# A transformer layer and a Mamba layer on one core: a new order inside the Mamba pair step, and the weighting of x on GpSimd

## What is computed

```python
gate, hbc, dt = split(hidden @ in_proj_w)
hbc = silu(causal_conv4(hbc) + conv_b)          # x (4096 channels), B, C (128 each)
dt  = softplus(dt + dt_bias);  dA = dt * -exp(A_log);  cum = cumsum(dA)   # inside a block
scores = (C_i . B_j) * exp(cum_i - cum_j) * dt_j          # i >= j
Y_diag = scores @ x
states = sum_l exp(cum_last - cum_l) * dt_l * B_l x_l     # of each block
state  = exp(cum_last) * state + states                   # carried from block to block
Y_off  = exp(cum_l) * C_l @ state_before
hidden = (Y_diag + Y_off + D * x) * silu(gate)
out    = rmsnorm(hidden) * norm_w @ out_proj_w
```

## Time and profile before

| | |
|---|---|
| median of 3 runs | 1969.08 us (1966.39 to 1969.34) |
| the profiled execution's own time | 1966.99 us |
| its span, first to last instruction | 1965.2 us |
| mean granted TensorE clock | 0.994 |
| busy: TensorE, VectorE, ScalarE, GpSimd | 1911.9, 1532.6, 1310.2, 830.7 us |
| DMA, mean over the span | 122 GB/s |

### The profile page before, as it was taken

How to read it: one execution, slowest core, us unless ns; L and a number is a source line. 1 busy time by engine, 2 the same in 40 slices (tenths; PEclk the granted TensorE clock), 3 DMA queues, 4 the chain that set the end, 5 groups by cost and what they waited for, 6 DMA issues and landing times.

```text
span 1965.2 us, 43300 instructions
## 1 busy us (share of the span) xinstructions
PE 1911.9 (97%) x12642; PEld 1607.5 (82%) x12642; DVE 1532.6 (78%) x2860; ACT 1310.2 (67%) x2983; POOL 830.7 (42%) x997
## 2 busy tenths in 40 slices
PE   7999999999999999999999999999999999999998
PEld 7888778888888968888878886888888888788886
DVE  6886678888788468888878836888888883688886
ACT  4663389999555148888845514888875551588885
POOL 2210268888200016777710001777770000177776
PEclk9999999999999999999999999999999999999999
DMA  6330356656422114444422211544442221244442
GB/s 231 120 120 1 124 162 207 203 193 208 134 75 85 52 46 156 146 155 148 164 77 84 75 62 35 168 146 157 146 153 86 91 62 49 83 146 156 146 153 78
DMA packets 122051, 239.86 MB, mean 122 GB/s; under 512 B 10832, under 2 KB 48912, under 8 KB 121872
## 3 DMA queue, kind: packets, MB, share of 16 engines
q1 hardware_dynamic: 122000, 239.18, 37.2%
HBM read 198.37 MB, written 37.62 MB: 120 GB/s over the span
## 4 chain that ended last, share of the span: by engine, by line
PE 71%; issue 20%; DVE 5%; ACT 2%; POOL 1%; DMA 0%; POOLq 0%; DVEq 0%; ACTq 0%
PE bank L695 31%; PE bank L965 12%; PE bank L952 6%; PE bank L941 5%; PE bank L932 4%; PE bank L924 3%; PE both L695 2%; PE bank L845 2%; PE bank L802 2%; DVE conv_acc L1428 1%; PE both L802 1%; PE bank L772 1%; PE bank L777 1%; PE bank L854 0%; ACT bank L1166 0%
## 5 line engine op out<-in xcount | busy, mean ns | idle before, releaser
L695 PE MATMUL bank<-xn_r,w_r 128*128 128x512 f32 x2268 | 610.6, 409 | 4.2 <-issue 3.2
L695 PEld LDWEIGHTS bank<-xn_r,w_r 128*128 128x128 f32 x2268 | 413.1, 189 | 104.9 <-issue 27.2
L1428 DVE SCALAR_TENSOR_TENSOR conv_acc<-bank,conv_sb,conv_acc 128x511 f32<-128x511 f32 (+2 forms) x408 | 304.3, 746 | 39.0 <-ACT conv_acc L1161 5.3
L570 POOL TENSOR_TENSOR rstd<-var_eps,minus_half 128x4 f32<-128x4 f32 (+2 forms) x12 | 9.7, 808 | 627.9 <-DVE var_eps L1357 627.9
L965 PE MATMUL bank<-wo_n,place 128*128 128x256 f32 x1024 | 255.1, 392 | 1.6 <-DVE place L1606 1.6
L1344 DVE TENSOR_TENSOR place_r<-bank,place_r 128x512 fp32r<-128x512 f32 (+1 forms) x320 | 186.7, 632 | 76.2 <-ACT place_r L1084 76.2
L1084 ACT ACTIVATE place_r<-bank 128x512 fp32r<-128x512 f32 (+1 forms) x320 | 159.2, 556 | 126.0 <-PE bank L695 98.7
L591 POOL TENSOR_TENSOR shared<-shared,c_t 128x768 f32<-128x768 f32 x128 | 234.4, 1831 | 6.6 <-ACT shared L1262 6.6
L965 PEld LDWEIGHTS bank<-wo_n,place 128*128 128x128 f32 x1024 | 184.0, 189 | 43.2 <-issue 21.2
L613 POOL TENSOR_TENSOR sumsq<-sumsq,place 128x512 f32<-128x512 f32 x127 | 161.9, 1275 | 114.8 <-ACT place L1150 114.8
L695 PE MATMUL bank<-place_r 128*128 128x512 f32 (+3 forms) x960 | 188.9, 337 | 8.4 <-DVE place_r L1344 6.0
(11 more groups left out here) (163 smaller groups left out, 3597.0 us busy)
## 6 DMA issues: line engine op xcount, KB each, us to landing
place_r<-cum_rows SPq DMA_DIRECT2D x128, 512.0 KB, 3.9
w_r<-pair_split SPq DMA_DIRECT2D x96, 512.0 KB, 3.7
w_r<-qkv_split SPq DMA_DIRECT2D x48, 512.0 KB, 4.0
pair_split<-w_r SPq DMA_DIRECT2D x32, 512.0 KB, 4.0
qkv_split<-w_r SPq DMA_DIRECT2D x16, 768.0 KB, 3.9
w_r<-qkv_split SPq DMA_DIRECT2D x48, 256.0 KB, 3.2
wo_n<-out_split SPq DMA_DIRECT2D x96, 128.0 KB, 3.6
raw<-in_w_pair SPq DMA_DIRECT2D x32, 256.0 KB, 3.9
```

What stands on the lines that cost most here:

```text
L695: ins = mm(out, lhsT=w(a), rhs=m(b), start=(start and i == 0), stop=(stop and i == 2), **kw)
L1428: stt(out=conv_acc[:, back:W], in0=src[:, 0:W - back], scalar=conv_sb[:, ch, TAPS - 1 - back:TAPS - back], in1=conv_acc[:, back:W], op0=AL ...
```

## The change

TensorE's order in a pair becomes project_gate(n+1), project_x(n+2), turn_x(n+1), project_out(n-1), in_block(n), off_block(n), make_states(n+1). The transposed x goes to one bank, ScalarE copies it to `x_raw` in SBUF, and GpSimd forms from it both x_w (`weigh_x`, now with the decays times dt) and x_dt (the new `weigh_dt`); VectorE's `weighted` is gone. The growth factors are made once per sequence by one exponential, saved to memory, and loaded spread over the partitions for each pair (`grow_save`, `grow_load`); ScalarE's `growth` is gone. The orders on ScalarE, VectorE, GpSimd and SyncE are rewritten to go with it; the raw weights of the first sequence are now split three pairs ahead of pair n in place of two. `c_grow` gets memory of its own. The diff, cut; lines with @@ name the engine:

```diff
-        c_grow = shared[:, n_mix + n_xw:n_mix + n_xw + 4 * (W - P)].rearrange("p (a h w) -> p a h w", a=2, h=2)
+        x_raw = shared[:, f_at + 4 * W:f_at + 5 * W].rearrange("p (t q) -> p t q", t=NT)
+        c_grow = sb("c_grow", [P, 2, 2, W - P])
...
@@ SyncE @@
+            def grow_save(b):
+                sp.wait_ge(s_grow_ev, b + 1)
+                sp.dma_start(grow_rows[bass.ds(b, 1), :, :].rearrange("b h w -> h (b w)"), square[0:MH, :]).then_inc(s_grow_saved, 16)
+                sp.wait_ge(s_grow_saved, b * 16 + 16)
+            def grow_load(b, n, par):
+                if not first(b) or not isinstance(n, int) or n > 0:
+                    sp.wait_ge(s_off_done, b * NPAIR + n)
+                sp.dma_start(c_grow[:, par, :, :], grow_rows[bass.ds(b, 1), bass.ds(n * 2, 2), P:W]
+                             .to_broadcast([P, 2, W - P])).then_inc(grow_in[par], 16)
...
-                    sp.wait_ge(s_grow_ev, b * NPAIR + n - 1)
+                    sp.wait_ge(s_span, b * NPAIR + n - 1)
...
-                with sp.Fori(1, NPAIR // 2 - 1) as i:
+                with sp.Fori(1, NPAIR // 2 - 2) as i:
                     for par in range(2):
-                        pair_save(i * 2 + par, par)
-                        pair_load(i * 2 + par + 2, par)
+                        grow_load(0, i * 2 + par + 1, 1 - par)
+                        pair_save(i * 2 + par + 1, 1 - par)
+                        pair_load(i * 2 + par + 3, 1 - par)
                         spread_load(0, i * 2 + par + 2, par)
                         out_save(i * 2 + par - 2, par)
                         out_load(i * 2 + par, par)
...
                         pair_fetch(i * 2 + par + 2, par)
                         spread_load(b, i * 2 + par + 2, par)
                         out_fetch(b, i * 2 + par, par)
+                        grow_load(b, i * 2 + par + 1, 1 - par)
...
@@ GpSimd @@
             def weigh_x(b, n, par):
-                pool.wait_ge(s_xdt_ready, N + 2)
+                pool.wait_ge(s_x_copied, N + 1)
                 pool.wait_ge(s_state_done, N + 1)
                 pool.tensor_tensor(x_w.rearrange("p c (h q) -> p c h q", h=2),
-                                   x_dt[:, par, 0:NT - 1, :].rearrange("p c (h q) -> p c h q", h=2),
+                                   x_raw[:, 0:NT - 1, :].rearrange("p c (h q) -> p c h q", h=2),
...
+            def weigh_dt(b, n, par):
+                pool.wait_ge(s_x_copied, N + 1)
+                if not isinstance(n, int) or n > 1:
+                    pool.wait_ge(s_off_done, N)
+                pool.tensor_tensor(x_dt[:, par, :, :].rearrange("p t (h q) -> p t h q", h=2),
+                                   x_raw.rearrange("p t (h q) -> p t h q", h=2),
+                                   dt_sb[:, :, bass.ds(n * 2, 2)].unsqueeze(3).to_broadcast([P, NT, 2, HD]),
+                                   ALU.mult).then_inc(s_xdt_ready, 1)
             def weigh_c(b, n, par):
-                pool.wait_ge(s_grow_ev, b * NPAIR + n + 1)
+                pool.wait_ge(grow_in[par], (b * NPAIR + n - par + 2) * 8)
...
-                def pair(n, par, ahead, before=2):
-                    if before > 1:
-                        add_squares(b, n - 2)
+                def prepare(n, par):
                     weigh_x(b, n, par)
+                    weigh_c(b, n, par)
+                    weigh_dt(b, n, par)
+                def pair(n, par, ahead, before=1):
+                    carry_states(b, n)
                     if ahead and first(b):
-                        split_low(NH + n + 2, par, 2 * D)
-                    weigh_c(b, n, par)
-                    carry_states(b, n)
+                        split_low(NH + n + 3, 1 - par, 2 * D)
+                    if before > 0:
+                        add_squares(b, n - 1)
+                    prepare(n + 1, 1 - par)
...
+                pool.tensor_tensor(dec[:, 0:NT - 1, :], dec[:, 0:NT - 1, :], dt_sb[:, 0:NT - 1, :], ALU.mult).then_inc(s_dec_dt, 1)
...
@@ TensorE @@
-                for bk, t0 in ((0, 0), (2, 2)):
-                    for t in (t0, t0 + 1):
-                        ins = pe.transpose(bank[bk][:, t * P:(t + 1) * P], xs[:, par, t * P:(t + 1) * P], ident[:])
-                    ins.then_inc(s_x_turned, 1)
+                for t in range(NT):
+                    ins = pe.transpose(bank[2][:, t * P:(t + 1) * P], xs[:, par, t * P:(t + 1) * P], ident[:])
+                ins.then_inc(s_x_turned, 1)
...
-                    if before > 0:
-                        turn_x(b, n, par)
-                        off_block(b, n - 1, 1 - par)
...
-                    if more:
-                        project_gate(b, n + 1, 1 - par)
-                    make_states(b, n, par)
...
-                    in_block(b, n, par)
-                    if before > 0:
-                        project_out(b, n - 1, 1 - par, isinstance(n, int) and n == 1, False)
-                    if ahead:
-                        project_x(b, n + 2, par)
+                    if more:
+                        project_gate(b, n + 1, 1 - par)
...
+                    if ahead:
+                        project_x(b, n + 2, par)
                     if more:
+                        turn_x(b, n + 1, 1 - par)
+                    if before > 0:
+                        project_out(b, n - 1, 1 - par, isinstance(n, int) and n == 1, False)
...
                     in_block(b, n, par)
+                    off_block(b, n, par)
+                    if more:
+                        make_states(b, n + 1, 1 - par)
+                make_states(b, 0, 0)
...
@@ ScalarE @@
+            def copy_x(b, n):
+                N = b * NPAIR + n
+                act.wait_ge(s_x_turned, N + 1)
+                act.wait_ge(s_xdt_ready, N + 1)
+                copy_out(x_raw.rearrange("p t q -> p (t q)"), bank[2][:], s_x_copied)
...
+                A(square, neg_cum, ACT.Exp, scale=-1.0).then_inc(s_grow_ev, 1)
...
-                def growth(n, par):
-                    A(c_grow[:, par, :, :], spread[:, par, :].rearrange("p (h w) -> p h w", h=2)[:, :, P:W], ACT.Exp,
-                      scale=-1.0).then_inc(s_grow_ev, 1)
...
                     act.wait_ge(s_state_done, N + 2)
                     act.wait_ge(s_off_done, N + 1)
                     copy_out(state[:].rearrange("p c q -> p (c q)"), bank[2][:, 0:W - P], s_state_ev)
                     if more:
-                        mixes(n + 1, 1 - par)
                         act.wait_ge(s_state_ev, N + 2)
                         conv_tanh(K + n + 3, bank[2])
-                        growth(n + 1, 1 - par)
                     if not begin:
                         squares(b, n - 1)
+                    if more:
+                        gate_tanh(b, n + 1, 1 - par)
+                        if deep and first(b):
+                            w_high(NH + n + 3, 1 - par, 2 * D)
+                        if ahead:
+                            pair_conv_start(b, n + 2)
+                        copy_x(b, n + 1)
+                        mixes(n + 1, 1 - par)
+                        if ahead:
+                            spans(n + 2, par)
...
@@ VectorE @@
-            def weighted(b, n, par):
-                for half, (bk, t0) in enumerate(((0, 0), (2, 2))):
-                    dve.wait_ge(s_x_turned, N * 2 + half + 1)
-                    tt(x_dt[:, par, t0:t0 + 2, :].rearrange("p t (h q) -> p t h q", h=2),
...
                     if not begin:
-                        weighted(b, n, par)
                         base, gated = tail(n - 1, 1 - par)
                         base()
                         gated()
                     if more:
-                        if not begin:
-                            conv_taps(K + n + 3, ch, bank[1])
-                            dve.wait_ge(s_hid_ready, N + 1)
+                        conv_end(K + n + 3, xs[:, 1 - par, :], bank[2])
+                    mixed(b, n, par)
+                    if more:
                         pair_gate(b, n + 1, 1 - par)
-                        conv_end(K + n + 3, xs[:, 1 - par, :], bank[2])
-                        mixed(b, n + 1, 1 - par)
+                        if ahead:
+                            conv_taps(K + n + 4, n + 2 if isinstance(n, int) else bass.ds(n + 2, 1), bank[1])
```

More of the change, by code:

```diff
@@ L485, in first_sequence @@
                         out_load(i * 2 + par, par)
-                for par in range(2):
-                    pair_save(NPAIR - 2 + par, par)
-                    out_save(NPAIR - 4 + par, par)
-                    out_load(NPAIR - 2 + par, par)
+                for n in range(NPAIR - 4, NPAIR):
+                    par = n % 2
+                    if n + 1 < NPAIR:
+                        grow_load(0, n + 1, 1 - par)
+                        pair_save(n + 1, 1 - par)
+                    if n + 3 < NPAIR:
+                        pair_load(n + 3, 1 - par)
+                    if n + 2 < NPAIR:
+                        spread_load(0, n + 2, par)
```

(51 more changed lines are left out.)

67 lines of the change are left out of this document (41 added, 26 removed).

## The result

| | before | after |
|---|---|---|
| median, us | 1968.15 (4 runs, 1966.39 to 1969.34) | 1995.74 (4 runs, 1990.71 to 1998.23) |
| span of the profiled execution | 1965.2 | 1996.4 |
| mean granted TensorE clock | 0.994 | 0.984 |
| mean pair, first sequence (pairs 2 to 30) | 7.81 | 9.77 |
| mean pair, each later sequence | 7.81 | 7.49 |

The changed kernel is slower: ratio 1.0142, 95% interval 1.0124 to 1.0160. The forecast was 1958 us, 1944 to 1984. A pair is counted from states product to states product on TensorE; the means run from the states of pair 2 to those of pair 30, counted from 0, which is 28 distances.

The account below looks back on a forecast made before the run. TensorE bounds the pair loop; SyncE's wait would bound the changed first sequence. From 1966.99 us, -30.5 for sequences 2 to 4 and +21 for the first gave 1958 us, range 1944 to 1984.

Parts of the forecast that it names:

- The excursion: TensorE's pair: entering and leaving the 128*64 tile costs 0.36 us; grouping in and off saves one, 7.81 to 7.45.
- The later sequences: Sequences 2 to 4: 31 x 0.36 us gained in each, less 1.0 for the start; -30.5 us together.
- GpSimd's weigh dt: New GpSimd product forming x_dt, put at 1.11 us, between 0.83 and 1.28.
- rival 2: GpSimd becomes the bound in all sequences, its jobs and hand-overs at 7.66 us a pair; 1985 us, chance 0.20.
- rival 3: In and off side by side still pay both excursions, so only the costs stay; 1992 us, chance 0.08.
- GpSimd's sum in the first sequence: GpSimd's work per first-sequence pair with weigh dt on top of the split: 8.35 us, ends 8.1 and 8.55.
- The wait that makes the first sequence slow: SyncE's in-order queue: the growth load waits for off(n-1), delaying the raw weights behind it; 8.6 us a pair, +21 us.
- the sum of the first sequence's round: From off(n-1) to off(n+1), two pairs: 5.7 + 4.4 + 7.1 = 17.2 us, so 8.6 a pair.
- Pairs over 9.1 us: Stated sign: first-sequence pairs under 8.1 or over 9.1 us would make the forecast wrong.
- last off product to ScalarE's high part: First sequence: product tail, SyncE's issues and the raw load's landing of 3.9 to 4.0; 5.7 us, ends 5.4 and 6.4.
- high part, split, squares, weigh x to the states: First sequence, ScalarE then GpSimd: high part, split, squares, weigh x and hand-overs; 4.4 us.
- states to the last off product: First sequence, TensorE: states, gate and x, turn, out, entry, in and off up to the last; 7.1 us.

Follow-up runs that it names:

- e5: e1 with TensorE doing project_out(n-1) between in_block(n) and off_block(n) in all sequences; 1989.4 us, ratio 1.0127 to the kernel before.
- e1: Changed kernel, but in the first sequence SyncE issues the growth load last in its round; 1946.1 us, ratio 0.9896 to the kernel before.
- e8: Changed kernel without growth rows by transfer: ScalarE makes them behind the gate's tanh; 1950.9 us, ratio 0.9926 to the kernel before.
- e4: Changed kernel plus 12 extra TensorE products before every odd pair's states in the first sequence; 1983.2 us, ratio 1.0087 to the kernel before.
- e3: Changed kernel, but from pair 3 of the first sequence the growth load brings 32 of 384 columns; 1986.8 us, ratio 1.0105 to the kernel before.
- e6: e1 with VectorE instead of GpSimd forming x_dt in the first sequence; 1933.9 us, ratio 0.9842 to the kernel before.

## Why the prediction was wrong

**What was right.** The excursion: 0.36 us forecast, 7.81 - 7.49 = 0.32 measured for the change, at most 0.36 for its undoing in e5. The later sequences: -30.5 forecast, -27.1 measured. GpSimd's weigh dt: 1.11 forecast, 1.05 measured. GpSimd at 88% in the second sequence, with pairs of 7.49, puts rival 2 out, and the one long 128*64 stretch in these pairs puts rival 3 out. GpSimd's sum in the first sequence: 8.35 forecast (ends 8.1 and 8.55) as the floor under the wait, 8.09 measured in e1. VectorE and ScalarE do not hold up the later sequences: TensorE is busy 210.59 of 211 us there. The wait that makes the first sequence slow is the one named: SyncE's order, as e1 and e8 show.

**The step that failed is the sum of the first sequence's round**, "two pairs: 17.2 us, so 8.6 a pair; ends 8.45 and 8.95". Pairs over 9.1 us were its own sign of being wrong, and they take 9.77. The mechanism is there as put; two of its three terms were mis-sized:

| term | forecast | measured in the round 458.46 to 478.43 |
|---|---|---|
| last off product to ScalarE's high part | 5.7 (5.4 to 6.4) | 474.38 - 467.34 = 7.04 |
| high part, split, squares, weigh x to the states | 4.4 | 478.43 - 474.38 = 4.05 |
| states to the last off product | 7.1 | 467.34 - 458.46 = 8.88 |
| sum | 17.2 | 19.97 |

In the first, I took the landing of the raw load as 3.9 to 4.0, from its median in the kernel before; here it takes 5.0, in the middle of a burst that begins with the growth load. Of the 1.3 us, 0.3 are issue and 1.0 landing. In the third I laid TensorE's instructions end to end at the full clock. The forecast's own round has 14.9 us of TensorE work in 17.2, so the idle time had to come in one piece before the states; I named that wait and did not ask what TensorE does after it. In this round its clock falls to 0.5 and gives 1.6 of the 1.75 us (states 1.18 in place of 0.69, gate and x 3.97 in place of 2.86).

This round has both excesses; the four at the full clock have only the first. With 8.6 forecast and 9.77 measured over 28 pairs the loop is 33 us longer than forecast. About 13 of them are the clock's, by the ten rounds of 1.3 us, and most of the other 20 the raw load's.

What the first sequence cost in all is 58 us against the 21 forecast. The 4 to 5 us of that miss that the pairs leave over lie behind its last states. From there to the first states of the second sequence it is 799.34 - 552.42 = 246.9 us, and was 740.97 - 499.42 = 241.6; TensorE idles 2.9 us before 556.24, and its granted clock is 0.67 over the next 4.1. What it waits for there was not traced. The later sequences add the 3.4 us that they stayed behind. Together that is the miss of 40 us of the profiled execution, 38 at the median.

**The ends of the range.** 8.95 was set by a longer burst alone. The first term's 7.04 lies outside its own ends of 5.4 and 6.4, and the third had no ends. The side of the result hung on both: the gain of one part and the loss of the other were sized as near neighbours, 30.5 and 21, and the loss was 58.

## What to carry to other kernels

When a transfer with a new, late wait goes into a queue that is served in order, count how far ahead each transfer behind it was issued before: that lead is what the wait takes away, and putting the waiting transfer last in the round may give it all back (here 50 us, for the same bytes and the same waits). A landing time is a price only for a queue that looks the same around the transfer: the raw load landed in 3.9 and 4.0 us where the spread load followed it 5 us later, and in 4.7 to 5.3 where it followed at once. And where a sum leaves TensorE one long idle stretch per round, what follows it may run at half its clock, as here in ten rounds of 14: price it before choosing the bound.

## What the runs showed of the hardware that was not expected

- After a gap of 3.45 us TensorE took 1.18 us for the states products in place of 0.69, and 3.97 for gate and x in place of 2.86, at a granted clock of 0.60 and then 0.50. Extra products in the gap kept it at 1.00 and made the kernel faster (e4). The gap's length alone does not tell: in the changed kernel the clock stayed at 1.00 after 3.35 us (361.49), and in e3 it fell after 2.02 us (460.76; gate and x then took 4.42).
- A VectorE product of 128x512 with both inputs in SBUF and a GpSimd product of 128x768 that fell together did not share the time: the one that started first, by as little as 0.01 us, ran at its usual length (0.68 or 1.83 us), and the other took 2.28 to 2.39 us (e6). The Trainium skill, GPSIMD Engine Reference, section Specifications, says that the two engines share their SBUF interfaces and contend when VectorE's instruction has two SBUF inputs; these rows agree. The kernel before had that product read PSUM, and its 256-element halves stayed at 0.42 us beside GpSimd's squares.
- Going in and out of the 128*64 tile cost 0.32 to 0.36 us together. The Trainium skill, TensorEngine Tiling (Array Packing), section Key Properties, says that a change of the tiling mode drains the engine; the change and e5 agree with it as far as the time stands at those borders.
